# Selective-scan mixer in a fused four-layer network: the product that drives the scan, computed by VectorE straight from PSUM in one flat loop over 64 states

## The reference

```python
ssm_params = jnp.einsum('btd,ed->bte', x_conv, x_proj_w)
B_ssm = ssm_params[..., :N]                       # N = 16 states
C_ssm = ssm_params[..., N:2 * N]
dt = jax.nn.softplus(ssm_params[..., -1:] * dt_proj_w[None, None, :, 0] + dt_proj_b)
A = -jnp.exp(A_log)
dA = jnp.exp(dt[..., None] * A[None, None])
dBx = dt[..., None] * B_ssm[:, :, None, :] * x_conv[..., None]
def step(h, inp):
    dA_t, dBx_t, C_t = inp
    h = dA_t * h + dBx_t
    y_t = jnp.einsum('bdn,bn->bd', h, C_t)
    return (h, y_t)
y = y * jax.nn.silu(z)
return jnp.einsum('btd,ed->bte', y, out_proj_w)
```

## Time and profile before

| | |
|---|---|
| median of 3 runs | 1349.36 us (1343.19 to 1352.21) |
| profiled execution, first to last instruction | 1359.7 us |
| mean granted TensorE clock in it | 0.908 of full |
| busy: TensorE, VectorE, ScalarE, GpSimd | 1121.5, 721.7, 502.6, 212.4 us |
| first scan to end of last sum into x of this mixer | 876.6 to 1029.3 us |
| in that stretch busy: TensorE, VectorE, ScalarE, GpSimd | 108.4, 144.8, 76.8, 117.9 us |

### The profile page before, as it was taken

How to read it: one execution, slowest core, us unless ns; L and a number is a source line. 1 busy time by engine, 2 the same in 40 slices (tenths; PEclk the granted TensorE clock), 3 DMA queues, 4 the chain that set the end, 5 groups by cost and what they waited for, 6 DMA issues and landing times.

```text
span 1359.7 us, 14092 instructions
## 1 busy us (share of the span) xinstructions
PE 1121.5 (82%) x4232; PEld 520.0 (38%) x4232; DVE 721.7 (53%) x1435; ACT 502.6 (37%) x937; POOL 212.4 (16%) x151
## 2 busy tenths in 40 slices
PE   4898989898889898998929638567677899998577
PEld 2445454544233333434316413122224344444233
DVE  4413131333978787853504323599995455554544
ACT  2213221223356565674204304755542222225410
POOL 9000000000000000000440170297770000000000
PEclk7699999999699999999959858798988899999779
DMA  7400000011021212121015320000000000000001
GB/s 175 136 0 1 0 0 0 0 45 32 18 60 36 60 36 59 36 78 49 24 36 152 89 53 1 0 0 1 0 0 1 0 0 0 0 0 0 1 0 31
DMA packets 60067, 41.16 MB, mean 30 GB/s; under 512 B 16830, under 2 KB 57648, under 8 KB 59668
## 3 DMA queue, kind: packets, MB, share of 16 engines
q1 hardware_dynamic: 57972, 37.11, 10.1%
q0 software_dynamic: 2048, 3.47, 1.0%
HBM read 29.49 MB, written 11.53 MB: 30 GB/s over the span
## 4 chain that ended last, share of the span: by engine, by line
PE 60%; issue 14%; DVE 10%; ACT 5%; POOL 4%; SPq 2%; another core or an unknown queue 2%; DMA 1%; POOLq 0%; DVEq 0%; ACTq 0%
PE psum L540 59%; POOL sb_scr L531 4%; ACT sb_scr L1246 3%; DVE sb_scr L1722 2%; DVE sb_scr L1570 1%; ACT L1246 1%; DVE sb_scr L1984 1%; DVE sb_small L1685 1%; PE psum L1022 1%; SPq L337 1%; DMA sb_down<-L_ffn_w_down 0%; PE psum L1004 0%; DVE sb_h L1575 0%; DVE sb_scr L1625 0%
## 5 line engine op out<-in xcount | busy, mean ns | idle before, releaser
L1246 ACT ACTIVATE sb_scr<-psum 128x512 f32<-128x512 f32 (+4 forms) x656 | 328.4, 538 | 585.1 <-PE psum L540 460.2
L540 PE MATMUL psum<-sb_h,sb_wide 128*128 (+1 forms) x448 | 224.5, 607 | 0.0
L1722 DVE TENSOR_REDUCE sb_scr<-psum 128x1 f32<-128x512 f32 x256 | 164.1, 685 | 40.1 <-PE psum L540 39.2
L540 PE MATMUL psum<-sb_scr,sb_wide 128*128 128x512 f32 x256 | 132.2, 598 | 5.9 <-DVE sb_scr L2060 5.9
L531 POOL TENSOR_TENSOR sb_scr<-sb_dtx_now,sb_scr 128x512 f32<-128x512 f32 x64 | 119.2, 1888 | 86.3 <-ACT sb_scr L1246 85.1
L509 POOL DMA_INDIRECT expert_in<-sb_scr x32 | 31.3, 979 | 636.4 <-DVE sb_scr L1888 626.9
L540 PEld LDWEIGHTS psum<-sb_h,sb_wide 128*128 128x128 f32 x448 | 85.4, 195 | 98.2 <-issue 97.9
L540 PE MATMUL psum<-sb_wparts,sb_pick 96*128 (+1 forms) x192 | 76.0, 420 | 54.2 <-DVE sb_scr L1994 40.6
L1667 DVE TENSOR_SCALAR sb_scr<-psum,sb_b 128x512 f32<-128x512 f32 x48 | 36.0, 751 | 151.6 <-PE psum L540 151.6
L540 PE MATMUL psum<-sb_kstack,sb_qstack 96*128 96x512 bf16 x256 | 104.5, 414 | 13.0 <-DVE sb_scr L1722 12.9
L1984 DVE TENSOR_TENSOR_SCAN sb_scr<-sb_scr 128x512 f32<-128x512 f32 x64 | 106.4, 1666 | 5.5 <-ACT sb_scr L1246 4.4
(11 more groups left out here) (228 smaller groups left out, 1400.4 us busy)
## 6 DMA issues: line engine op xcount, KB each, us to landing
sb_qstack<-q_bounce SPq DMA_DIRECT2D x48, 96.0 KB
sb_kstack<-k_bounce SPq DMA_DIRECT2D x144, 32.0 KB
expert_in<-sb_scr SPq DMA_DIRECT2D x2, 1280.0 KB, 7.8
sb_scr<-expert_in SPq DMA_DIRECT2D x8, 320.0 KB, 3.4
expert_out<-sb_scr SPq DMA_DIRECT2D x8, 320.0 KB, 2.7
sb_wide<-L_ffn_W SPq DMA_DIRECT2D x2, 1024.0 KB, 6.8
q_bounce<-sb_scr SPq DMA_DIRECT2D x12, 128.0 KB, 2.4
k_bounce<-sb_scr SPq DMA_DIRECT2D x12, 128.0 KB, 2.4
```

Of the source, the lines that this page charges most:

```text
L540: return nc.tensor.matmul(out_, w, r, start=start, stop=stop, **kw)
L1246: return nc.scalar.activation(out_, in_, func, **kw)
L1722: v.reduce_max(headmax[:, g % 2, t, j:j + 1], bank(i % ring), AX.X).then_inc(sem("maxed"), 1)
```

## The change

VectorE computes the drive product itself, one instruction D for each state, that reads B from the PSUM bank and `dtx` of the batch from SBUF. GpSimd's product, ScalarE's copies into `bcast_b` and into `dtx_now`, and the waits between them are gone. In TensorE's program B of state n+2 now stands where B of state n stood, behind a wait for D of state n, since D is what frees the bank. VectorE's turn is D of state n+1, S of state n, R of state n-1. The loops over batches 1 to 3 are written out on TensorE, VectorE and ScalarE. The gate of the batch before stands one turn later on VectorE. The rings in the scratch buffer move up, and `read` keeps its two buffers.

```diff
-            with pool.Fori(0, NB) as b:
-                for n in range(NSTATE):
-                    if n == 0:
-
-                        pool.wait_ge(sem("dtx_taken"), b + 1)
-
-                    pool.wait_ge(sem("b_spread"), b * NSTATE + n + 1)
-                    if n >= RB:
-
-                        pool.wait_ge(sem("scanned"), b * NSTATE + n - RB + 1)
-                    nc.gpsimd.tensor_tensor(drive[:, n % RB, :], dtx_now[:], bcast_b[:, n % RB, :], ALU.mult).then_inc(sem("drive_ready"), 1)
...
-            def states(b, begin):
+            def spread_b(b, n):
+
+                mm(bank(n % 2), pick[:, n, :], wparts[:, b, :]).then_inc(sem("b_done"), 1)
+
+            def states(b, begin, last):
                 for n in range(NSTATE):
-                    if n >= 2 or not begin:
-
-                        pe.wait_ge(sem("b_spread"), b * NSTATE + n - 1)
-                    mm(bank(n % 2), pick[:, n, :], wparts[:, b, :]).then_inc(sem("b_done"), 1)
+                    if n + 2 < NSTATE or not last:
+
+                        pe.wait_ge(sem("drive_ready"), b * NSTATE + n + 1)
+                        spread_b(*((b, n + 2) if n + 2 < NSTATE else (b + 1, n + 2 - NSTATE)))
                     if n >= RC or not begin:
 
                         pe.wait_ge(sem("read_ready"), b * NSTATE + n - RC + 1)
...
-            def states(b, begin):
-                if not begin:
-
-                    act.wait_ge(sem("drive_ready"), b * NSTATE)
-                f(dtx_now[:], dtx[:, b, :], ACT.Copy).then_inc(sem("dtx_taken"), 1)
+            def decays(b, begin):
                 for n in range(NSTATE):
-                    r = n % RB
-                    act.wait_ge(sem("b_done"), b * NSTATE + n + 1)
                     if n >= RB or not begin:
 
-                        act.wait_ge(sem("drive_ready"), b * NSTATE + n - RB + 1)
                         act.wait_ge(sem("scanned"), b * NSTATE + n - RB + 1)
-                    f(bcast_b[:, r, :], bank(n % 2), ACT.Copy).then_inc(sem("b_spread"), 1)
-                    f(decay[:, r, :], dt[:, b, :], ACT.Exp, scale=a_neg[:, n:n + 1]).then_inc(sem("decay_ready"), 1)
...
+            def drive_in(b, n):
+                i = b * NSTATE + n
+                dve.wait_ge(sem("b_done"), i + 1)
+                v.tensor_tensor(drive[:, n % RB, :], bank(n % 2), dtx[:, b, :], ALU.mult).then_inc(sem("drive_ready"), 1)
+
...
+            drive_in(0, 0)
+            for i in range(NB * NSTATE + 1):
+                b, n = divmod(i, NSTATE)
+                if n == RC - 1 and b >= 1:
+                    gate_batch(b - 1, False)
+                if i + 1 < NB * NSTATE:
+                    drive_in(*divmod(i + 1, NSTATE))
+                if i < NB * NSTATE:
+                    scan(b, n, b == 0)
+                if i >= 1:
+                    read_state(*divmod(i - 1, NSTATE), i <= NSTATE)
+                if n == 2 * RC and b >= 1:
+                    add_batch(b - 1)
```

More of the change, by code:

```diff
@@ L248, in build @@
         RB, RC = 4, 4
-        decay, drive, bcast_b, state = (ring(6144 + RB * S * n, RB) for n in range(4))
-        read = ring(6144 + 4 * RB * S, 2)
+        drive, decay, state = (ring(6144 + RB * S * n, RB) for n in range(3))
+        read = ring(6144 + 3 * RB * S, 2)
         xw, gx, ga, dec, drv, st3 = (batches(NB * S * n) for n in range(6))
@@ L1124, in states @@
                         add_state(b - 1, NSTATE + n - RC)
-            states(0, True)
-            with pe.Fori(1, NB) as b:
-                states(b, False)
+            spread_b(0, 0)
+            spread_b(0, 1)
+            for b in range(NB):
+                states(b, b == 0, b == NB - 1)
             for n in range(NSTATE - RC, NSTATE):
@@ L1457, in _ @@
             act.wait_ge(sem("dtx_ready"), NB)
-            def states(b, begin):
-                if not begin:
-                    act.wait_ge(sem("drive_ready"), b * NSTATE)
-                f(dtx_now[:], dtx[:, b, :], ACT.Copy).then_inc(sem("dtx_taken"), 1)
+            def decays(b, begin):
                 for n in range(NSTATE):
-                    r = n % RB
-                    act.wait_ge(sem("b_done"), b * NSTATE + n + 1)
                     if n >= RB or not begin:
-                        act.wait_ge(sem("drive_ready"), b * NSTATE + n - RB + 1)
                         act.wait_ge(sem("scanned"), b * NSTATE + n - RB + 1)
-                    f(bcast_b[:, r, :], bank(n % 2), ACT.Copy).then_inc(sem("b_spread"), 1)
-                    f(decay[:, r, :], dt[:, b, :], ACT.Exp, scale=a_neg[:, n:n + 1]).then_inc(sem("decay_ready"), 1)
-            states(0, True)
-            with act.Fori(1, NB) as b:
-                states(b, False)
+                    f(decay[:, n % RB, :], dt[:, b, :], ACT.Exp, scale=a_neg[:, n:n + 1]).then_inc(sem("decay_ready"), 1)
+            for b in range(NB):
+                decays(b, b == 0)
             def copy_parts(k, at):
```

1 line of the change is left out of this document (removed).

## The result

| | before | after |
|---|---|---|
| median of the timed runs | 1346.34 us (1343.19 to 1352.21) | 1465.07 us (1452.94 to 1476.79) |
| ratio, 95% interval | | 1.081 (1.074 to 1.088) |
| profiled span | 1359.7 us | 1465.7 us |
| first scan, last scan (starts) | 876.6, 1022.0 | 862.2, 1120.1 |
| 63 turns between them | 145.3 us | 257.9 us |

The change made the kernel 8.1% slower. Predicted were 1459 us, and 256.5 us for the 63 turns. The 1349.36 us that the forecast was counted from is the median of three of the four runs of before.

What follows compares the result with a forecast made beforehand. VectorE was taken to bound the stage before, then a once-a-turn wait loop with TensorE mostly at half clock. The 63 turns gain 111.2 us, the start wins 1.2, net +110: 1459 us, range 1385 to 1472.

Steps and rivals of the forecast that it cites:

- VectorE's own work: VectorE's three instructions a turn, R 0.58, S (the scan) 1.13, D 0.58: 2.29 us against 2.15 steady before.
- The wait: R waits for A, queued on TensorE behind the new wait for D: 2.87 us a turn at full clock, 4.18 at half.
- the chain: Once a turn: end of D, matmuls B, C, A, then R, next D; 2.87 us at full clock, 4.18 at half.
- R's idle time: VectorE's idle time before R, ended by TensorE: some 0.6 us a turn at full clock, 1.9 at half.
- The clock: TensorE starts the stage at half clock and stays there, save some turns behind the three output projections inside the loop.
- the 8 turns put at full clock: Of 60 turns in the stage, 8 estimated at 2.87 us, 23.0 us in all; the other 52 at 4.18.
- the first three turns: Turns of the stage with no A to wait for: 3 x 2.29 = 6.9 us.
- The swinging clock: Rival: half of the 60 turns at each TensorE clock level, +81 us, 1430 us; chance 0.17.
- the full clock: Rival: the waits as forecast but TensorE at full clock throughout, +38 us, 1388 us; chance 0.11.
- The sum: The stage's 63 turns take 256.5 us against 145.3, +111.2; net +110, profiled span 1470, median 1459 us.
- The start: Ahead of the first scan, table load and decay come right behind `dtx`: 1.2 us won.

Runs made afterwards that it cites:

- e1: The changed kernel with four buffers of `read` in place of two; 0.999 of the kernel before, median 1360.1 us, 148.0 us from first to last scan.
- e2: The changed kernel with the sum matmul A and the output projection issued ahead of B and C on TensorE; 1.005 of the kernel before, 1370.3 us.
- e5: The changed kernel with ScalarE's copy of B kept, D reading it and TensorE's B waiting for that copy; 1.007 of the kernel before, 1368.6 us.
- e7: The changed kernel with matmul C issued ahead of TensorE's wait for D; 1.062 of the kernel before, 1446.3 us.
- e3: The changed kernel with four redundant copies of matmul C ahead of TensorE's wait for D; 1.024 of the kernel before, 1394.8 us.
- e6: The changed kernel with four `read` buffers and the odd states' drive product back on GpSimd, from ScalarE's copy; 0.993 of the kernel before, 1351.8 us.
- e4: The kernel before, GpSimd's product and copies kept, with only the loops over batches 1 to 3 written out; 0.999 of before, 1357.5 us.

## Why the prediction was right

**VectorE's own work.** Forecast 2.29 a turn, shown by e1 to be 2.31: D 0.60 rather than 0.58, S 1.13, R 0.58. Scans of 1.21 throughout, as forecast. The gate and the sum into x cost 0.60 each (turns of 2.91 in e1).

**The wait.** Forecast as the chain end of D, B, C, A, R, D. Three experiments take one link away each and the chain is gone (e1 the reuse of `read`, e2 A's place behind the wait, e5 the wait for D). e7 takes one term out and the turn falls by this term. The terms: 2.87 forecast and 2.90 measured at full clock, since D is 0.68 until its end and not the 0.66 that I took from R. At half clock 4.18 forecast and 4.18 measured, with the same 0.02 too little for D made up by B and C, which took 0.83 (893.73 to 894.56) and not 0.85. R's idle time was put at 1.9 and 0.6 and is 1.76 and 0.49: the rows count it from the end of S, which lies 0.08 behind its pitch.

**The clock.** This was the step with the least ground, and the rows on both sides of it were given. It held: 0.52 in the stage. Of the 8 turns put at full clock there were 3, the third projection bringing none. 5 turns at 1.31 are 6.6 us. In the first three turns 6.3 us were measured against 6.9, and the last two, 2.31 and 1.71, do not wait for A at all, which the sum had left out: 4.3 us less than forecast. So the total is nearer than its parts: 6.6 too little and 4.9 too much nearly cancel, and that is luck. e3 shows the clock to be a cause and not a companion: with full clock and the chain kept, the kernel costs 2.4% and not 8.1%. That divides the loss: about 71 us of the stage are the half clock (257.9 - 187.0). About 42 are what is left at full clock (187.0 - 145.3), 2.7 of them VectorE's own work by e1 (148.0) and the rest the chain.

**Rivals.** The swinging clock and the full clock did not come about. The rule of the Trainium skill (TensorE: Matmul & The Clock Gate, Loop structure matters more than you think), that VectorE's reads between the groups leave TensorE's clock alone, is given there for a loop whose next matmuls follow at once. Carried over to this chain, where TensorE waits for VectorE once a turn, it did not hold: with 1.44 us idle of 4.18 the clock stayed at half, and with 1.44 of 2.90 it fell from full, twice. In e1, where TensorE idles 0.84 us before a turn's matmuls, the clock fell three times and came back, 0.92 in the mean.

**The sum.** Stage +112.6, forecast +111.2. Profiled span 1465.7, forecast 1470. The start: the first scan begins 1.12 us after `dtx` is finished (862.18 - 861.06), 3.22 before, so 2.1 were won instead of 1.2; ScalarE had loaded its table while it waited. The profiled spans differ by 106.0 only: between the first instruction and the first scan, in code that is the same, the profile after took 12.3 us less than these 2.1 explain, and behind the last scan 7.8 more. The first is scatter of unchanged code: e5 and e6, with the same code up to the stage, have their first scan at 885.9 and at 865.0. The stretch behind the last scan lay between 337.7 and 342.7 us in the profiles of before and e1 to e7, and was 345.6 after. Whether the change has a part in these last microseconds is not shown.

## What to carry to other kernels

When work moves to the engine that bounds a stage, add up not only its busy time but the order of waits: if the first instruction in another engine's turn now waits for the bounding engine, everything behind it in that queue waits too, and a buffer released from there can close a loop that runs once a turn. Two cures are cheap and both were enough here, more buffers for the tile whose release closes the loop, or the releasing instruction ahead of the new wait. A loop between TensorE and another engine can cost twice, as it did here, once for the wait and once for the clock that the idle gaps leave low. A second engine's work that slows a scan can be placed beside instructions that read PSUM (e6).

## What the runs showed of the hardware that I had not expected

- TensorE with more to do was quicker: four redundant matmuls in a gap of 1.44 us brought the granted clock from 0.52 to 0.97 and took 71 us off the stage (e3).
- GpSimd's product and VectorE disturbed each other only while VectorE ran the scan, with its two operands in SBUF. Beside R and D, one operand in PSUM, the product kept its 1.27 and they their 0.66 and 0.68. The expectation of e6 was built on this. New is that one of the two waits and they do not share: where one had clearly begun before the other, the later one was lengthened. A row of e6 with nearly the whole product under a scan:

```profile
876.46 1.27 POOL L527 TENSOR_TENSOR sb_scr<-sb_scr 128x512 f32<-128x512 f32 x1 [3.70 <-ACT sb_scr L1247]
876.65 2.16 DVE L1989 TENSOR_TENSOR_SCAN sb_scr<-sb_scr 128x512 f32<-128x512 f32 x1
```

  The product took 1.27 and the scan 2.16, which is 1.21 and most of the 1.08 that the product still had to go. Two of the 32 products of e6 were lengthened themselves. One began at 865.63 under a scan that had begun at 865.03: the product took 1.69 and the scan 1.22. The other began at 924.84, level with a scan at 924.86, and took 2.28, while that scan kept its 1.21 and the next one, at 926.57, took 1.64. In the kernel before both are long, 1888 ns for the product and 1666 for the scan in the mean.
- The turns at a batch's end, 3.2, 2.2 and 3.3 us, were the same with the loop instructions and without (e4).
- The start of the stage, in unchanged code, lay between 862 and 886 us over the profiled executions, which is more than the whole gain of e6. What sets it was not tried. The two profiles with the earliest starts, e6 and after, had TensorE's granted clock at 0.92 and 0.91 over what lies ahead of the stage, the three latest, e2, e3 and e5, had 0.90; that these belong together is not shown.
